# Waiting for each eight scattered transfers in a graph network kernel

## The reference, cut to what matters

```python
x = layernorm(x + L0(x))   # 3 rounds: m = h @ W; agg = segment_sum(m[src], dst); h = gru_cell(agg, h)
x = layernorm(x + L1(x))   # two segment sums over the edges with degree weights, batch norm, relu
x = layernorm(x + L2(x))   # attention over the edges, softmax by src
x = layernorm(x + L3(x))   # MLP on [x[src], x[dst]] per edge, segment_sum over dst, MLP per node
```

## Time and profile before

| | us |
|---|---|
| median of 3 runs | 4744.27 |
| lowest and highest | 4742.21, 4745.18 |
| span of the profiled execution | 7303.0 |
| the profiled execution's own time | not given apart from its span |
| PE, POOL busy in it | 4076.2, 2658.9 |
| second scatter (832 transfers), first to last start | 2156.0 to 3296.1 |

### The profile page before, as it was taken

The page is one execution under the profiler, slowest core; times in us unless marked ns, Lnnn a source line. Parts: engine busy times, 40 slices in busy tenths (PEclk is TensorE's granted clock), DMA queues, the critical chain, the costliest instruction groups (busy, mean ns, idle before and its releaser), DMA issues. The chain is left out here.

```text
span 7303.0 us, 82736 instructions
## 1 busy us (share of the span) xinstructions
PE 4076.2 (56%) x24237; PEld 3354.5 (46%) x24238; DVE 3381.7 (46%) x7886; ACT 2340.3 (32%) x3120; POOL 2658.9 (36%) x2706
## 2 busy tenths in 40 slices
PE   4332641019981111117989798988672197666655
PEld 2111420007761101106778586858571197665644
DVE  4222540358970000106788776456451076555545
ACT  0000010005640000004555455557461075444433
POOL 4555157730017777770000000000427601444463
PEclk7665865559995555558999898989785598888777
DMA  9400000009970000116658287843444343444432
GB/s 376 155 0 0 0 2 0 0 23 334 368 250 0 0 0 0 28 25 222 232 189 293 96 293 214 296 162 95 132 125 124 97 139 98 132 132 130 130 95 67
DMA packets 364823, 923.20 MB, mean 126 GB/s; under 512 B 114026, under 2 KB 138716, under 8 KB 364531
## 3 DMA queue, kind: packets, MB, share of 16 engines
q1 hardware_dynamic: 214722, 650.09, 26.9%
q10 hardware_dynamic: 58609, 180.13, 6.4%
q0 software_dynamic: 91200, 89.42, 5.2%
HBM read 705.69 MB, written 213.71 MB: 126 GB/s over the span
## 5 line engine op out<-in xcount | busy, mean ns | idle before, releaser
L1741 POOL DMA_INDIRECT edges_halves<-local,gather_idx x832 | 854.9, 1027 | 791.7 <-SPq L372 505.4
L1680 POOL DMA_INDIRECT adj_t<-cell_val,cell_at x832 | 828.6, 996 | 465.2 <-issue 369.9
L862 PE MATMUL ps<-tiles_r,stage_r 128*128 128x512 f32 x2028 | 811.6, 400 | 158.2 <-issue 132.0
L1134 POOL DMA_INDIRECT big<-table,gather_idx x576 | 548.4, 952 | 832.3 <-DVE stage L1284 376.3
L869 PE MATMUL ps<-stage,big 128*128 128x130 f32 x4046 | 520.1, 284 | 370.3 <-issue 354.7
L1134 POOL DMA_INDIRECT x_fm<-table,gather_idx x384 | 370.2, 964 | 959.8 <-DMA table<-cell_at 689.7
L869 PEld LDWEIGHTS ps<-stage,big 128*128 128x128 f32 x4046 | 497.9, 199 | 388.5 <-issue 384.6
L2059 PE MATMUL ps<-big,ident_h 128*128 128x104 bf16 (+1 forms) x2880 | 359.7, 256 | 460.4 <-issue 459.7
L1253 PE MATMUL ps<-big,stage 128*128 x1920 | 356.2, 342 | 352.7 <-issue 189.3
L1319 PE MATMUL ps<-ident,big 128*128 128x128 f32 x260 | 73.3, 377 | 817.2 <-issue 768.2
L2442 DVE TENSOR_TENSOR big<-ps,stage 128x1248 bf16<-128x1248 f32 x192 | 270.7, 1451 | 519.5 <-remote 385.1
(11 more groups left out here) (482 smaller groups left out, 9007.8 us busy)
## 6 DMA issues: line engine op xcount, KB each, us to landing
onehot<-adj_t SPq DMA_DIRECT2D x332, 512.0 KB
big<-adj_t SPq DMA_DIRECT2D x332, 512.0 KB
onehot<-adj_s SPq DMA_DIRECT2D x170, 512.0 KB
adj_t<-rows ACTq DMA_DIRECT2D x13, 6656.0 KB
adj_s<-big ACTq DMA_DIRECT2D x157, 512.0 KB, 5.3
stage<-local_rows SPq DMA_DIRECT2D x120, 512.0 KB
big<-adj_s SPq DMA_DIRECT2D x84, 512.0 KB
x_fm<-adj_s SPq DMA_DIRECT2D x84, 512.0 KB
```

Of the source, the lines that this page charges most:

```text
L862: nc.tensor.matmul(psum_fm(p, n)[:, 0:cut], upper_rows[:, k, :], tile[:, 0:cut], start=k == 0, stop=False, skip_group_check=True)
L1134: return nc.gpsimd.indirect_dma_start(out, None, table[0:N, :], bass.IndirectOffsetOnAxis(gather_idx[:, t:t + 1], 0))
L1680: nc.gpsimd.indirect_dma_start(out, bass.IndirectOffsetOnAxis(cells[:, c:c + 1], 0), cell_val[:, c:c + 1], None).then_inc(S(name), 16)
L1741: nc.gpsimd.indirect_dma_start(edges_halves, bass.IndirectOffsetOnAxis(slot_at[:, at:at + 1], 0), slot_val[:, at:at + 1], None).then_inc(h ...
```

## The change

In the second scatter GpSimd issues eight transfers, waits until these have landed, and only then issues the next eight. Before, it issued freely and waited, 16 transfers into each slab, for the slab before. The wait for the slab before moves from column 16 to column 0 of the next slab.

```diff
+BURST = 8
+assert SLW % BURST == 0
...
             for n in range(SL):
                 for c in range(SLW):
-                    if n and c == SC:
-                        sorted_there(n - 1)
+                    if c % BURST == 0:
+                        if c:
+                            wait(pool, halves_written[n % 2], 16 * (SLW * (n // 2) + c))
+                            pool.sem_inc(rows_opened, 1)
+                        elif n:
+                            sorted_there(n - 1)
                     at = n * SLW + c
                     nc.gpsimd.indirect_dma_start(edges_halves, bass.IndirectOffsetOnAxis(slot_at[:, at:at + 1], 0),
                                                  slot_val[:, at:at + 1], None).then_inc(halves_written[n % 2].sem, 16)
```

## The result

| | us |
|---|---|
| before, median of 4 runs | 4743.88 (4742.21 to 4745.18) |
| after, median of 4 runs | 4889.32 (4888.77 to 4891.74) |
| ratio | 1.0304, 95% interval 1.0292 to 1.0316 |
| span of the profiled execution after | 4889.9 |

The kernel became 145 us slower. The forecast was 4821 (77 us slower), and its range reached to 4900. So the sign and the mechanism came out as forecast. The size did not: the loss is almost twice the 77 us.

A forecast was written before the change was run, and what follows sets the result against it. The scatter was taken as hidden up to 1318.7 us from its start, delaying DVE in pass 4 beyond that. With bursts it would end at 1396, 77 us late: 4744 + 77 = 4821 us, range 4738 to 4900.

The forecast's parts named there:

- The stretched recording: Profiled execution, 7303.0 us against 4744.27 timed: timed runs were inferred to go at the pace of the dense stretches.
- The cover: Other engines' work beside the second scatter: 1282.1 us until "third" opens, 1330.5 until DVE comes to `pair_keys`.
- What the profile after would show: 103 idle entries of about 2.0 us, more in pass 1; L1746 still waiting long for L372; exposure seen only in timed runs.
- Hidden before, and its length: Second scatter before the change: 1143 us with its last landing, hidden up to 1318.7 us, 176 us to spare.
- rival 2: Second scatter already exposed before the change, each wait paid in full: 4923 to 5078 us; chance 0.05.
- Bursts outside passes: GRU loops and norm beside the scatter: 12.0 us for a burst with its wait, 27.3 bursts.
- The price of a wait in a pass: GpSimd's wait beside tile loads: 3.24 us, bounds 1.74 and 5.8.
- the prediction's own sum: Second scatter: 27.3 and 67.2 bursts by "third", 9.5 left take 114 us; it ends at 1396, 77 past 1318.7.
- the 1.5 us: Surcharge on a wait in a pass above the quiet 1.74, from packets one to two transfers behind at pass 1's start.
- rival 3: Passes 1 and 2: fewer outstanding transfers let tile loads run faster, at most 13 us gained, 4731 us; chance 0.07.
- Rival 1: Second scatter stays hidden, its sum under 1318.7 us: 4744 us, no change; chance 0.38.

The follow-up runs named there:

- bursts of 4: Changed kernel with bursts of four transfers in place of eight, 207 waits: 5146.59 us, ratio 1.0852.
- the last half: Changed kernel with bursts of eight only in slabs 4 to 7, earlier slabs waiting only at their start, 55 waits: 4748.11 us, ratio 1.0006.
- the pairs needed later: Changed kernel with DVE's pair steps and PE's turning of the pairs moved from group 0 to group 4 of pass 4: 4802.27 us, ratio 1.0129.
- three quarters: Changed kernel with bursts of eight only in slabs 0 to 5, 79 waits: 4802.16 us, ratio 1.0121.
- bursts of 16: Changed kernel with bursts of sixteen in place of eight, 55 waits: 4739.47 us, ratio 0.9994.
- both halves: Two kernels, the changed one with bursts only in slabs 0 to 3 (4738.87 us) or only in slabs 4 to 7 (4748.11 us).

## Why the prediction was right, and what was mis-sized

**The stretched recording: right.** The inference that the timed runs go at the dense stretches' pace carried the forecast, and the second profile of the kernel before shows it: 4740.6 us of span in place of 7303.0. The cover put together from dense stretches gave 1282.1 us to "third" and 1330.5 to DVE's arrival. In that second profile "third" opens 1310.3 us after the scatter's start (SyncE's next transfer at 2537.47, less 1227.2) and DVE comes after 1355.6. After the change they come at 1303.3 and 1348.9. The cover was thus estimated 18 to 28 us too short. It was taken from passes with no scatter beside them, 318 us each. Passes 1 and 2 take longer with the scatter beside them: from their first product to the end of their last, 331.5 us each in the second profile, 328.0 and 326.7 after the change. Pass 3 doesn't: it takes 318 us in both, with the scatter beside its first 117 us in the one and beside all of it in the other. PE at the start and the end of pass 2, in the second profile, then after the change:

```profile
1750.78 0.77 PE L862 MATMUL ps<-tiles_r,stage_r 128*128 128x512 f32 x1 [8.20 <-ACT tiles_r L797]
...
2081.86 0.40 PE L864 MATMUL ps<-tiles_r,lower_r 128*128 128x512 f32 x1
```
```profile
1747.23 0.77 PE L864 MATMUL ps<-tiles_r,stage_r 128*128 128x512 f32 x1 [8.35 <-ACT tiles_r L799]
...
2073.55 0.40 PE L866 MATMUL ps<-tiles_r,lower_r 128*128 128x512 f32 x1
```

**What the profile after would show: one sentence wrong.** It was expected that the profile after would be stretched too, and that L1746 would still show a long wait. It was recorded undisturbed, so the exposure stands in it openly.

**Hidden before, and its length: right within 33 us.** Forecast 1143 us with the last landing and 176 us of slack. It takes 1110 with 233 of slack. The interval over the whole scatter is 1107.0 / 831 = 1.332 in place of 1.372. So rival 2, exposed already before, is out. In the second profile of the kernel before GpSimd's single instructions last 0.970 us at the median and 1.492 at most. The Trainium skill (SBUF — State Buffer, A bandwidth-pool intuition that's wrong (but worth ruling out)) has a GpSimd transfer go from 620 ns to some 3100 beside a VectorE copy; no instruction here grows like that. The most that one gains, 0.5 us, is less than one of VectorE's casts in the passes takes (0.69 us), and no run here shows whether a lock is behind it.

**Bursts outside passes: right.** Forecast were 12.0 us a burst and 27.3 bursts up to "third"; the change shows 64 transfers, 8 bursts, between 1226 and 1322, so 12.0, and 64 + 67 + 89 = 220 transfers, 27.5 bursts, in the three stretches outside passes. The three together are 340 us and not 327, so it is 12.4 us a burst over all of them, and the count agrees as well as it does because both are larger. A quiet wait costs 1.95 - 0.30 = 1.65 where 1.74 was forecast.

**The price of a wait in a pass: the term that was mis-sized.** The forecast took 3.24 us, between bounds of 1.74 and 5.8. It is 4.7 - 0.30 = **4.4**. The three passes hold 167 + 174 + 162 = 503 transfers, 62.9 bursts of 15.3 us, in place of the forecast 67.2 of 14.2. Counting those that lie on a border of two stretches once, 720 of the 832 have been issued when "third" opens, and 112, 14.0 bursts, are left in place of 9.5. Put into the prediction's own sum, 4.4 in place of 3.24 gives 15.4 us a burst in a pass, 14.7 bursts left and 140 us in place of 77, so this term carries most of the miss; the long wait below is the rest. The step that failed is that the 1.5 us was read from how far GpSimd's queue fell behind at a pass's start. That tells how late packets are taken up, but not how late the last is finished. In the changed kernel it can be looked at directly. GpSimd's DMA queue from 2322.23 to 2323.23, from there to 2324.23, to 2325.23 and to 2326.52, right behind the issue of a burst's eighth transfer in pass 3 (packets, MB, and the time that the packets took as a share of the 16 engines' time):

```profile
q0 software_dynamic: 26, 0.00, 1.8%
...
q0 software_dynamic: 34, 0.00, 2.5%
...
q0 software_dynamic: 22, 0.00, 1.5%
...
q0 software_dynamic: 2, 0.00, 0.1%
```

And the same right behind an eighth issue in the hole, 2692.69 to 2693.69; in the rest, until the next issue, the queue moves nothing:

```profile
q0 software_dynamic: 32, 0.00, 2.4%
```

The two issues around each, on POOL's timeline:

```profile
2321.26 0.97 POOL L1747 DMA_INDIRECT edges_halves<-local,gather_idx  x1 [0.30 <-issue]
2326.52 1.08 POOL L1747 DMA_INDIRECT edges_halves<-local,gather_idx  x1 [4.29 <-DMA edges_halves<-local,gather_idx]
```
```profile
2691.72 0.97 POOL L1747 DMA_INDIRECT edges_halves<-local,gather_idx  x1 [0.30 <-issue]
2694.63 0.97 POOL L1747 DMA_INDIRECT edges_halves<-local,gather_idx  x1 [1.95 <-DMA edges_halves<-local,gather_idx]
```

Quiet, a transfer's 32 packets are through within 1 us, and for the last 0.94 us before the next issue the queue is empty. Beside the tile loads 84 packets, more than two transfers, are still on their way at the end of the eighth issue, and it takes 3 us until all but two are through. In these microseconds the packets of the load queue q1 alone take 77 to 95% of the engines' time. So here nearly the whole surplus is packets that come through late beside the loads. The rows show it for one wait; that the others in passes have the same cause is argued from the equal means of the three passes (4.66 to 4.77), not shown. The estimate of 3.5 us by the Trainium skill (DMA: Bandwidth & Descriptors, Latency and other measured facts) was nearer than 3.24 and still too low; the measured 4.4 decides.

**One wait that no one foresaw.** Beside "third" stands one wait of 19.75 us on POOL's timeline, and at 2530.12 SyncE had issued a store:

```profile
2560.58 0.97 POOL L1747 DMA_INDIRECT edges_halves<-local,gather_idx  x1 [19.75 <-DMA edges_halves<-local,gather_idx]
```
```profile
2530.12 0.40 SPq L1571 DMA_DIRECT2D degree_row<-small  x1
```

The DMA view of 2530 to 2560, the engines' busy tenths in 40 slices of 0.75 us, then queue by queue:

```profile
DMA  0476636759999999999996995502000000000000
...
q1 hardware_dynamic: 6672, 0.03, 75.7%
q0 software_dynamic: 256, 0.00, 4.4%
```

The store moves 26 KB in some 6,670 packets of 4 bytes, and the engines work on it until about 2551, 21 us from its issue; the time of its packets comes to 75.7% of the 30 us of all engines. Then the profile shows no packet on any engine, and still the wait lasts until 2560.58. So of the 19.75 us some 10 lie beside the store's packets, and over 9 lie behind the last packet of any queue, where a quiet transfer needs about 1.2 (its packets are through some 0.7 us after the issue, and the wait ends at 1.95). The same place shows a longest wait of 22.1 us with bursts of 4, 20.0 with the last half and 19.8 with the pairs needed later, each ending 4 to 7 us behind the last packet, and 6.8 with three quarters, whose last wait ends at 2489.29, ahead of this store. That the store is the cause is read from these rows; no kernel moved or removed it, and what the quiet end of the wait waits for stays open.

**The sum with measured terms.** The scatter ends, with its last landing, 1491.5 us after its start where 1396 was forecast. Of the 95 us some 54 are 4.5 more bursts left at "third" (at 12.0), 18 the long wait (19.75 less a quiet 1.95), and 21 the later "third". The longer cover takes 18 back, and 77 us late becomes 154. The later "third" and the longer cover all but cancel, so what is left is the dearer waits in passes and the long wait. Of these 145 arrive in the time. 7 us of the difference can be seen: DVE comes to `pair_keys` at 2575.7 in place of 2582.8. They are gained in passes 1 and 2 (3.5 and 4.8 us shorter). Pass 3 has no part in it: PE is busy for 312.50 us in the 315 from 2211, where pass 3 starts after the change, and in the kernel before, where it starts 7 us later, for as long from there:

```profile
2218.00:2533.00 315.00, 312.15 (x1341) 254.16 (x1342) 221.24 (x497) 176.88 (x169) 92.07 (x85) 0.98 0.85 288
```

This is rival 3's direction. Its size is not settled: the kernel that needs the pairs later is the same up to "third", and there "third" opens 1296.8 us after the scatter's start, 6.5 earlier than in the changed kernel, so that single profiles differ by as much as the 7 us. With bursts of 4 it opens after 1294.2. That fewer transfers beside the passes are the reason was not tested by itself.

**The rivals.** Rival 1, hidden, is what bursts of 16 and both halves show, and what the changed kernel would show with 233 us of growth or less. It fails here since the growth is 381.5. Rival 2 fails by the second profile, and rival 3 by sign.

## What to carry to other kernels

In this kernel a wait for the transfer just issued costs its landing time, 1.95 us with quiet DMA engines and 4.7 in the mean beside a stream of loads at 280 GB/s; the same wait one burst behind costs nearly nothing. Whether such waits cost time is settled by one subtraction: the length they add less the slack until the first engine on the path reads the result. Here the growth beyond the slack was paid almost one for one (53, 148 and 403 us cost 59, 145 and 403). If the profile's span and the timed runs are far apart, build the cover from the dense stretches, or take a second profile, before any row is believed.

## What the runs showed of the hardware that was not expected

- The same kernel was recorded once with a span of 7303.0 us and once of 4740.6. The stretch lay on the engines beside GpSimd's indirect transfers (PE's transposes 0.72 us apart there), while GpSimd's own instructions kept their 0.97 us.
- A wait for one small indirect write is not steady: 1.95 us at quiet engines, 4.7 in the mean beside tile loads (2.4 to 7.1), and 16 to 22 right behind pass 3, beside a 26 KB store in 6,672 packets. In the changed kernel that wait goes on for 9 us after the last packet of any queue.
- Pass 2 takes 317 us with no scatter beside it, 331.5 with one in the kernel before and 326.7 in the changed kernel; pass 3 takes 318 in both, though the scatter stands beside a third of it in the one and beside all of it in the other.
